# Chained VectorE stages cut into pieces of one link, and all engine orders replaced, in a two-layer gated stack

## The reference

```
x = x + tanh(g_xattn[0]) * L0_xattn(layernorm(x), ctx, mask)      # A
x = x + tanh(g_ffn[0])   * L0_ffn(layernorm(x))                   # F
x = x + tanh(g_xattn[1]) * L1_xattn(layernorm(x), ctx, ctx)       # B
x = x + tanh(g_ffn[1])   * L1_ffn(layernorm(x))                   # R, then the experts
```

## Time and profile before

| what | us |
|---|---|
| median of 3 runs (lowest, highest) | 1640.79 (1635.14, 1644.37) |
| the profiled execution itself | 1642.42 |
| its span, first to last instruction | 1640.8 |
| TensorE busy | 1400.4 (85%) |
| VectorE busy | 1117.3 (68%) |
| ScalarE busy | 993.4 (61%) |
| GpSimd busy | 413.3 (25%) |

### The profile page before, as it was taken

The page is one execution under the profiler, slowest core; times in us unless marked ns, Lnnn a source line. Parts: engine busy times, 40 slices in busy tenths (PEclk is TensorE's granted clock), DMA queues, the critical chain, the costliest instruction groups (busy, mean ns, idle before and its releaser), DMA issues.

```text
span 1640.8 us, 35711 instructions
## 1 busy us (share of the span) xinstructions
PE 1400.4 (85%) x11645; PEld 1072.6 (65%) x11646; DVE 1117.3 (68%) x2887; ACT 993.4 (61%) x2861; POOL 413.3 (25%) x560
## 2 busy tenths in 40 slices
PE   2567789989999889989998671999999999999994
PEld 1445556665666566656664430888888888888883
DVE  7977779899988999899986534344444454444452
ACT  1244778888888888888876760444445444455542
POOL 0101011211122211212111112334433444344442
PEclk9587999999999999999999975999999999999997
DMA  6020132112320223203220005551231412322214
GB/s 192 13 87 30 62 103 103 45 61 104 103 92 21 95 104 103 72 33 104 94 94 8 8 14 179 177 162 32 33 112 30 114 32 35 108 35 32 35 31 123
DMA packets 63158, 123.58 MB, mean 75 GB/s; under 512 B 13955, under 2 KB 51967, under 8 KB 58879
## 3 DMA queue, kind: packets, MB, share of 16 engines
q1 hardware_dynamic: 45743, 102.75, 18.0%
q0 software_dynamic: 17312, 19.56, 7.2%
HBM read 78.64 MB, written 48.04 MB: 77 GB/s over the span
## 4 chain that ended last, share of the span: by engine, by line
PE 52%; DVE 32%; ACT 8%; issue 5%; DMA 2%; POOL 1%; SPq 0%; DVEq 0%; ACTq 0%; POOLq 0%
PE bank L1401 15%; PE bank L1403 14%; PE bank L1402 14%; DVE b_mn L1121 4%; ACT b_ex L746 3%; PE bank L1483 2%; PE bank L1495 2%; DVE wm L1238 1%; DVE f_hs L1182 1%; DVE split_room L1265 1%; DVE wm L1190 1%; PE bank L1719 1%; DVE x L1176 1%; DVE wm L1196 1%; DVE wm L1201 1%
## 5 line engine op out<-in xcount | busy, mean ns | idle before, releaser
L1401 PE MATMUL bank<-split_room,wm 128*128 128x256 f16 x1152 | 314.9, 273 | 8.2 <-issue 6.8
L1378 DVE SCALAR_TENSOR_TENSOR split_room<-bank,b12e,split_room 128x256 f32<-128x256 f32 x288 | 138.2, 484 | 265.6 <-ACT split_room L900 260.8
L1402 PE MATMUL bank<-split_room,wm 128*128 128x256 f16 x1152 | 314.8, 273 | 0.0
L1403 PE MATMUL bank<-split_room,wm 128*128 128x256 f16 x1152 | 314.7, 273 | 0.0
L900 ACT ACTIVATE split_room<-bank,b12e 128x256 f32<-128x256 f32 x288 | 134.2, 470 | 196.0 <-PE bank L1403 194.2
L746 ACT ACTIVATE b_ex<-bank,b_mn 128x120 f32<-128x120 f32 x512 | 177.0, 361 | 36.9 <-DVE b_mn L1121 28.0
L1403 PE MATMUL bank<-wm,split_room 128*128 128x256 f16 x576 | 157.0, 273 | 0.0
L1401 PE MATMUL bank<-wm,split_room 128*128 128x256 f16 x576 | 157.0, 273 | 0.0
L1402 PE MATMUL bank<-wm,split_room 128*128 128x256 f16 x576 | 157.0, 273 | 0.0
L692 POOL DMA_INDIRECT acc<-split_room,m_cur x72 | 116.1, 1612 | 133.0 <-ACT split_room L914 106.1
L1483 PE MATMUL bank<-b_k,b_q 128*128 128x480 f32 x256 | 131.8, 597 | 14.6 <-ACT b_q L834 14.6
(11 more groups left out here) (356 smaller groups left out, 3616.3 us busy)
## 6 DMA issues: line engine op xcount, KB each, us to landing
split_room<-in_L_ffn_W SPq DMA_DIRECT2D x48, 512.0 KB, 8.0
wsplit<-split_room SPq DMA_DIRECT2D x16, 1536.0 KB, 6.6
wm<-wsplit SPq DMA_DIRECT2D x16, 1536.0 KB, 8.5
acc<-x SPq DMA_DIRECT2D x17, 256.0 KB, 2.2
xin<-in_x SPq DMA_DIRECT2D x16, 256.0 KB
rows<-r_row SPq DMA_DIRECT2D x16, 256.0 KB, 3.7
ct<-in_ctx SPq DMA_DIRECT2D x16, 120.0 KB
cb<-in_ctx SPq DMA_DIRECT2D x16, 120.0 KB, 2.6
```

What stands on the lines that cost most here:

```text
L1378: dve.scalar_tensor_tensor(m_h[:, c % 3], bank[c % 4][:, TILE:2 * TILE], b12e[:, p, 1, c:c + 1], m_s[:, c % 2], ALU.add, ALU.mult).then_in ...
L1401: pe.matmul(o, lh, rh, start=start, stop=False)
L1402: pe.matmul(o, ll, rh, start=False, stop=False)
L1403: return pe.matmul(o, lh, rl, start=False, stop=stop)
```

## The change

VectorE's stages that held a chain are cut so that each function holds the operations between two waits. A cut stage's pieces are entries of their own in VectorE's lists: A.ln with A.ln_1, _2, _3; F.ln, B.ln, R.ln with _1, _2; A.rk, A.r0, A.r1, A.p0, A.p1 with _1; F.q becomes F.qa, F.qa_1, F.qa_2, F.qb, and F.q0a, F.q1a get _1, _2; F.qc, F.q0c, F.q1c, F.p, F.p0, F.p1 get _1; R.logit gets _1 to _5; R.rank becomes R.rank_0 to R.rank_5 and R.rank, the last one a wait alone. Operations, operands and waits inside stay as they were. The lists FIRST, ORDER and LAST of all five engines are new. W0 to W2 of batch 15 no longer stand at the end of VectorE's list. The core of the diff, with TensorE's middle list and most of the first and last lists left out:

```diff
-            "ACT": ("A.z@0 A.t@0 A.s0@0 A.s1@0 A.t0@0 A.t1@0 W0@0 A.ot@0 P.n0@0 W1@0 A.z@1 A.t@1 P.n1@0 P.n2@0 P.n3@0 F.z@0 "
...
-            "DVE": ("A.ln@0 P.q0a@0 A.t@0 P.q0b@0 A.rk@0 A.r0@0 A.r1@0 A.s0@0 P.q0c@0 P.q0d@0 A.s1@0 P.q1a@0 P.q1b@0 A.p0@0 "
-                "A.p1@0 P.q1c@0 P.q1d@0 A.ot@0 P.q2a@0 A.out@0 A.ln@1 F.ln@0 P.q2b@0 P.q2c@0 A.t@1 P.q2d@0 A.rk@1 P.n0@0 "
-                "P.n1@0 A.r0@1 A.r1@1 P.n2@0 P.n3@0 P.n4@0 A.s0@1 W0@0 A.s1@1 F.q@0 P.n5@0 P.n6@0 W1@0 A.p0@1 A.p1@1 A.ot@1 "
...
-            "PE": ("A.t@0 A.kv@0 A.q0@0 A.q1@0 A.s0@0 A.s1@0 A.t0@0 A.t1@0 A.p0@0 A.p1@0 A.ot@0 P.n0@0 P.n1@0 A.out@0 A.t@1 "
...
+            "ACT": ("W0@0 P.n0@0 P.n1@0 P.n2@0 A.z@0 W1@0 A.t@0 P.n3@0 P.n4@0 P.n5@0 P.n6@0 A.s0@0 A.s1@0 A.t0@0 A.t1@0 A.ot@0 "
+                "A.z@1 P.n7@0 A.t@1 F.z@0 A.s0@1 F.a@0 A.s1@1 A.t0@1 A.t1@1 F.t@0 A.ot@1 F.gu0@0 F.gu1@0 F.gu2@0 W2@0 F.gu3@0 "
...
+            "DVE": ("P.q0a@0 P.q0b@0 A.ln@0 P.q0c@0 A.ln_1@0 P.q0d@0 P.q1a@0 P.q1b@0 P.q1c@0 P.q1d@0 A.ln_2@0 P.q2a@0 A.ln_3@0 "
+                "P.q2b@0 P.q2c@0 P.q2d@0 P.n0@0 P.n1@0 P.n2@0 A.t@0 P.n3@0 P.n4@0 P.n5@0 P.n6@0 A.rk@0 A.rk_1@0 A.r0@0 "
+                "A.r0_1@0 A.r1@0 A.r1_1@0 A.s0@0 P.b0@0 A.s1@0 A.p0@0 A.p0_1@0 P.b1@0 A.p1@0 A.p1_1@0 A.ot@0 W0@0 A.out@0 "
...
+            "PE": ("P.n0@0 P.n1@0 P.n2@0 A.t@0 P.n3@0 P.n4@0 A.kv@0 P.n5@0 P.n6@0 A.q0@0 P.n7@0 A.q1@0 A.s0@0 A.s1@0 A.t0@0 "
...
         ORDER = {
-            "SP": ("A.load/-1 B.load/1 B.out/3 W/0 R.rank/3").split(),
-            "POOL": ("F.ln/1 B.ln/2 R.ln/3 A.ln/-1 R.scatter/3").split(),
-            "ACT": ("F.a1/2 F.ht0/2 W0/1 B.t2/3 B.s3/3 W1/1 W2/1 B.t3/3 B.s4/3 F.ht1/2 B.s5/3 B.t4/3 B.s6/3 B.rx0/3 A.s0/0 B.r3/3 "
-                "F.z/1 B.t5/3 A.s1/0 B.o0/3 A.t0/0 F.a/1 A.t1/0 B.s7/3 B.t6/3 F.t/1 B.t7/3 B.rx1/3 B.r7/3 B.o1/3 A.ot/0 "
-                "F.gu0/1 B.z/2 B.ct/2 B.zt/2 R.z/3 F.gu1/1 R.t/3 F.gu2/1 A.z/-1 F.gu3/1 B.k/2 B.q/2 A.t/-1 F.a0/1 R.logit/3 "
-                "B.s0/2 B.s1/2 B.t0/2 B.s2/2 B.t1/2").split(),
-            "DVE": ("A.r0/0 B.s5/3 A.r1/0 F.ht1/2 B.s6/3 B.rx0/3 A.s0/0 F.ln/1 W0/1 B.p3/3 W1/1 A.s1/0 F.q/1 B.o0/3 B.s7/3 F.qc/1 "
-                "F.p/1 F.d1/2 A.p0/0 A.p1/0 B.rx1/3 F.t/1 W2/1 B.p7/3 B.ln/2 B.o1/3 A.ot/0 B.out/3 R.ln/3 F.gu0/1 A.out/0 "
-                "B.ct/2 A.ln/-1 F.gu1/1 F.q0a/1 F.gu2/1 B.zt/2 R.t/3 F.gu3/1 F.q0b/1 F.q1a/1 R.logit/3 A.t/-1 B.s0/2 B.v/2 "
-                "F.q0c/1 B.s1/2 F.p0/1 B.s2/2 F.q1b/1 R.rank/3 A.rk/-1 F.q1c/1 B.s3/2 F.p1/1 F.ht0/1 B.s4/2").split(),
...
+            "SP": ("A.load/-1 B.out/3 B.load/0 W/0 R.rank/3").split(),
+            "POOL": ("A.ln/-1 R.ln/3 F.ln/0 R.scatter/3 B.ln/1").split(),
+            "ACT": ("B.t1/3 F.ht0/2 B.t2/3 B.s3/3 F.ht1/2 B.t3/3 W0/1 W1/1 B.s4/3 B.s5/3 F.z/1 A.s0/0 B.t4/3 B.s6/3 B.rx0/3 F.a/1 "
+                "B.r3/3 A.s1/0 A.t0/0 B.t5/3 B.o0/3 A.t1/0 F.t/1 B.s7/3 A.ot/0 B.t6/3 F.gu0/1 B.t7/3 B.rx1/3 W2/1 B.r7/3 "
+                "B.o1/3 F.gu1/1 B.z/2 B.ct/2 F.gu2/1 A.z/-1 F.gu3/1 R.z/3 B.zt/2 F.a0/1 A.t/-1 B.k/2 B.q/2 R.t/3 F.a1/1 "
+                "B.s0/2 B.s1/2 R.logit/3 B.t0/2 B.s2/2").split(),
+            "DVE": ("B.o0/3 A.p0/0 B.s7/3 A.p0_1/0 A.p1/0 A.p1_1/0 F.t/1 B.rx1/3 W1/1 A.ot/0 B.ln/2 B.ln_1/2 B.ln_2/2 F.gu0/1 "
+                "A.out/0 A.ln/-1 B.p7/3 A.ln_1/-1 A.ln_2/-1 B.o1/3 F.gu1/1 A.ln_3/-1 F.q0a/1 B.out/3 F.q0a_1/1 R.ln/3 "
+                "F.q0a_2/1 R.ln_1/3 F.gu2/1 R.ln_2/3 B.ct/2 W2/1 F.gu3/1 F.q0b/1 F.q1a/1 B.zt/2 F.q1a_1/1 F.q1a_2/1 F.q0c/1 "
+                "A.t/-1 F.q0c_1/1 F.p0/1 F.p0_1/1 F.q1b/1 B.s0/2 B.v/2 R.t/3 R.logit/3 R.logit_1/3 F.q1c/1 B.s1/2 R.logit_2/3 "
+                "R.logit_3/3 R.logit_4/3 R.logit_5/3 F.q1c_1/1 A.rk/-1 B.s2/2 R.rank_0/3 R.rank_1/3 A.rk_1/-1 R.rank_2/3 "
+                "B.s3/2 F.p1/1 F.p1_1/1 F.ht0/1 R.rank_3/3 A.r0/-1 A.r0_1/-1 A.r1/-1 A.r1_1/-1 F.ht1/1 B.s4/2 R.rank_4/3 "
+                "B.s5/2 F.ln/0 F.ln_1/0 F.ln_2/0 R.rank_5/3 A.s0/-1 R.rank/3 B.s6/2 B.rx0/2 F.qa/0 F.qa_1/0 F.qa_2/0 F.qb/0 "
+                "W0/0 A.s1/-1 F.qc/0 B.p3/2 F.qc_1/0 F.p/0 F.p_1/0 F.d1/1").split(),
...
         }
...
-                "B.p7@15 B.o1@15 B.out@15 R.ln@15 R.t@15 R.logit@15 R.rank@15 W0@15 W1@15 W2@15").split(),
...
-                "B.s7@14 B.t6@14 B.p5@14 F.d0@15 F.d1@15 B.t7@14 B.p6@14 B.p7@14 B.out@14 B.ct@15 B.zt@15 B.k@15 B.q@15 "
...
+            "SP": ("B.out@13 R.rank@13 B.out@14 R.rank@14 B.out@15 R.rank@15").split(),
...
+                "F.gu1@15 B.z@14 B.ct@14 W2@15 F.gu2@15 B.zt@14 F.gu3@15 R.z@13 F.a0@15 B.k@14 B.q@14 R.t@13 F.a1@15 B.s0@14 "
...
+                "B.s6@14 R.rank_3@13 R.rank_4@13 B.rx0@14 F.d1@15 B.ln@15 B.ln_1@15 B.ln_2@15 B.p3@14 R.rank_5@13 R.rank@13 "
...
+                "R.rank_2@15 R.rank_3@15 R.rank_4@15 R.rank_5@15 R.rank@15").split(),
...
+                "B.s6@14 F.d1@15 B.s7@14 B.p3@14 B.p4@14 B.t5@14 B.t6@14 B.p5@14 B.t7@14 B.p6@14 B.ct@15 B.zt@15 B.p7@14 "
+                "B.out@14 B.k@15 B.q@15 B.v@15 B.s0@15 R.t@14 B.s1@15 R.logit@14 B.t0@15 B.s2@15 B.s3@15 B.p0@15 B.t1@15 "
...
             def variances(G, ch, source):
 
-                def stage(b, p):
-                    x_t, st, rv = G.x[:, p], G.st, G.rv
+                def stats(b, p):
                     ch.start(b)
                     dve.wait_ge(source.done, b + 1)
                     if not isinstance(b, int) or b >= 1:
                         dve.wait_ge(G.rsqrt, b)
                     for t in range(NT):
-                        ch.link(dve.bn_stats(st[:, t, 0:6], x_t[:, t]))
+                        ch.link(dve.bn_stats(G.st[:, t, 0:6], G.x[:, p, t]))
+
+                def moments(b, p):
+                    ch.go_on(b)
                     ch.hold()
                     for t in range(NT):
-                        ch.link(dve.bn_aggr(st[:, t, 6:8], st[:, t, 0:6]))
+                        ch.link(dve.bn_aggr(G.st[:, t, 6:8], G.st[:, t, 0:6]))
+
+                def guard(b, p):
+                    ch.go_on(b)
                     ch.wait()
-                    dve.tensor_scalar(rv[:, 0:NT], st[:, 0:NT, 7], 1e-5, None, ALU.add).then_inc(G.stats, 1)
-                return stage
+                    dve.tensor_scalar(G.rv[:, 0:NT], G.st[:, 0:NT, 7], 1e-5, None, ALU.add).then_inc(G.stats, 1)
+                return stats, moments, guard
...
-            def quantise_a(v, m, sc, b, n):
-                cf.link(dve.tensor_reduce(sc[:, 2], blocks(v), AX.X, ALU.max, apply_absolute_value=True))
-                cf.wait()
-                cf.link(dve.tensor_scalar(sc[:, 0], sc[:, 2], SIXTH, 1e-12, ALU.mult, ALU.max))
-                cf.wait()
-                dve.reciprocal(sc[:, 1], sc[:, 0]).then_inc(F.v, 1)
...
+            def f_largest(n):
+                v, m, sc = F_PARTS[n]
+
                 def stage(b, p):
                     cf.go_on(b)
-                    if part is quantise_a:
-                        dve.wait_ge(F.h, b * 4 + 2 * t + 2)
-                    part(f_h[:, t], f_hm[:, t], f_hs[:, t], b, 1 + t)
+                    if n == 0:
+                        dve.wait_ge(F.z, b + 1)
+                    else:
+                        dve.wait_ge(F.h, b * 4 + 2 * n)
+                    cf.link(dve.tensor_reduce(sc[:, 2], blocks(v), AX.X, ALU.max, apply_absolute_value=True))
+                return stage
+
+            def f_scale(n):
+                v, m, sc = F_PARTS[n]
+
+                def stage(b, p):
+                    cf.go_on(b)
+                    cf.wait()
+                    cf.link(dve.tensor_scalar(sc[:, 0], sc[:, 2], SIXTH, 1e-12, ALU.mult, ALU.max))
+                return stage
...
             def r_logit(b, p):
-
                 cr.go_on(b)
                 dve.wait_ge(R.lg_mm, b + 1)
                 dve.wait_ge(wB_in, 16 * 14)
                 cr.link(dve.tensor_tensor(r_lg[:, :, :], bank[5][:, 0:NT * NE].rearrange("p (t e) -> p t e", t=NT),
                                           br_s[:, :].unsqueeze(1).to_broadcast([P, NT, NE]), ALU.add))
+
+            def r_top_(b, p):
+                cr.go_on(b)
                 cr.hold()
                 for t in range(NT):
                     cr.link(dve.max(r_top[:, t], r_lg[:, t]))
+
```

154 lines of the change are left out of this document (105 added, 49 removed), and 98 rows, old and new, of tables (FIRST, LAST, ORDER).

## The result

The changed kernel takes **1677.74 us** (median of 4, 1675.64 to 1680.79) against 1639.09 for the kernel before in the same comparison (4 runs, 1635.14 to 1644.37): a ratio of **1.0238**, 95% interval 1.0217 to 1.0259. It is slower by 2.4%, where 1623 us (a ratio of 0.99) was forecast and 1643 was the upper end of the range. The profiled execution took 1680.8 us, with a span of 1679.2.

A forecast was written before the change was run, and what follows sets the result against it. TensorE (47.95 us busy) and VectorE (47.34) were taken to bound the 52.28 us step, neither saturated. Steps -21, start +8, drain -4.5 and handover -2 made -19.5 on 1642.4: 1623 us, range 1606 to 1643.

The forecast's parts named there:

- The steps: Eleven steady pipeline steps: each falls from 52.25 to 50.35 us, -21 us in all, bounds 0 and -32.
- busy sums stay: All engines: instructions and shapes are unchanged, so busy times stay and only distances and places move.
- The term of the links: VectorE's steps: 17 links get another piece in front, at 0.11 us each, 1.9 us a step.
- The rule weighed in the prediction: VectorE: the next operation waits for an empty pipe, so covered links give 0; rival of 1644 us, chance 0.05.
- The start: Up to B.out@1: weight preparation ahead of A.t@0 delays F.gu0@0 by 15, partly regained; net +8 us, bounds 0 and +18.
- The -7 for what no longer stands behind: Start, behind F.gu0@0: six pieces P.b, about 8 us together, no longer stand there, -7 us.
- The drain: Batches 13 to 15: B.ct@15 and B.zt@15 earlier on TensorE, plus batch 13's links; -4.5 us, bounds 0 and -9.
- The handover: Before the expert loop: batch 15's split comes earlier, SP sends its weights some 6 us earlier; -2 us, bounds 0 and -6.
- both move the same megabytes: Handover: both kernels load the same amount through the same SP queue, at DMA share 0.55, limiting the gain.
- the wait at L1354 shorter: Handover marker: VectorE's 9.65 us wait for the last split weights should shorten.
- F.z's wait: ScalarE's 1.76 us wait for F.ln's GpSimd operations at F.z: expected gone, booked at 0.
- the Exp load: ScalarE's 1.28 us table load moves from before R.logit to before B.s0; costed 0, otherwise 1.28 us a step.

The follow-up runs named there:

- e4_w2only: Changed kernel with W2 alone moved behind F.q1a in VectorE's step: 1635.6 us, ratio 0.9973.
- e2_oldw2: Kernel before, stages unsplit, with VectorE's W2 moved directly behind R.ln: 1652.4 us, ratio 1.0083.
- e1_split: Changed kernel's cut VectorE stages, with the kernel before's orders on every engine and each stage's pieces side by side: 1640.7 us, ratio 0.9999.
- e3_joinfill: Changed kernel with W2 and F.q0b behind F.q1a, VectorE's stage pieces rejoined (15 borders), B.k's products twice, A.kv's three times: 1693.5 us, ratio 1.0280.
- e3_table: Changed kernel with W2 and F.q0b behind F.q1a, P entries back beside A's stages, Silu in F's gate replaced by a copy: 1646.8 us, one execution.
- e5_both: Changed kernel with P entries back beside A's stages of batches 0 and 1, and W2 alone moved behind F.q1a: 1630.3 us, ratio 0.9906.
- e1_rz: Changed kernel with R.z moved behind B.zt in ScalarE's step, nothing else: 1661.8 us, ratio 1.0131.
- e4_kv: Changed kernel with A.kv's products computed twice on TensorE, nothing else: 1651.8 us, ratio 1.0072.
- e5_start: Changed kernel with P entries back beside A's stages of batches 0 and 1, steps as changed: 1653.0 us, ratio 1.0038.
- e3_w2fill: Changed kernel with W2 and F.q0b behind F.q1a, B.k's products computed twice and A.kv's three times: 1664.3 us, ratio 1.0103.

## Why the prediction was wrong, point by point

**The steps, forecast -21, measured +26.** Two of its own sentences failed.

The first is "W2 moves behind R.ln_2 and may slow R's operations by the same 0.9 us twice; R.z on ScalarE now has F.gu3 in front, which hides it; without that cover 1.8 us on R's chain, on which no later batch waits." The place was right and the size nearly: the two operations are 1.07 and 0.45 us longer. The cover failed: ScalarE was done with F.gu3 and waited 2.15 us. And the last clause was wrong. R's chain is awaited by nobody, but R.z is an **entry in ScalarE's queue**, and B.zt of the batch behind stands right behind it. That is 0.8 us a step (e4_w2only against the 51.9), some 9 us; in the old order the same place costs 1.1 (e2_oldw2 against e1_split).

The second is in the reading of the earlier trace rows, "at a full granted clock", from which TensorE's 47.95 us were taken as fixed ("busy sums stay"). The change leaves TensorE about as much idle time as before, but collects it: before, the longest wait was 0.88 us, after 1.96 and 1.80, with 2.9 us of work between them. The clock falls in every step, in ten of the eleven behind the second wait, and 54.67 less 51.9 is 2.8 us a step, **30 us**, more than all that the steps lost. No rival held this mechanism. VectorE's busy sum didn't stay either (47.34 to 46.16): an operation that starts before its forerunner's end is counted with it.

**The term of the links, 1.9 us a step.** The mechanism was right and the size too large. The kernel without both faults, e4_w2only, has steps of 51.09, 1.2 less than before, where 1.9 was booked; and 0.4 of the 1.2 come with the old orders as well (e1_split), so that 0.8 are left for the new ones. Against the forecast's 50.35 that is another 8 us, and the steps add up: -21 + 9 + 30 + 8 = +26. That covered links are worth something is shown by the other direction: uncovering 15 borders costs 2.4 (e3_joinfill), though a part of it is the pieces' later place. The rule weighed in the prediction (the Trainium skill, VectorE: DVE Perf Modes, "The DRAIN you can't avoid"), by which the semaphore costs nothing extra, is not borne out here: VectorE is busy 1.2 us more in the step with the 15 borders uncovered.

**The start, forecast +8 (0 to +18), measured +13.3.** A.t@0 came at 67.1 (69 forecast), F.gu0@0 at 133.5 (123 forecast), B.out@1 at 282.8 (278). The passes of A with little beside them were sized too short: A.t@0 to A.t@1 is 37.0 us, A.t@1 to F.gu0@0 29.3, where 24 + 8 and 22 were estimated. So F.gu0@0 is 25.5 us later than before, not 15. The -7 for what no longer stands behind was too small as well: from F.gu0@0 to B.out@1 it is 149.3 us for 161.5, -12.2. Two errors of 10 and 5 us took each other back in part, and that 13.3 lies in the range is partly luck.

**The drain, forecast -4.5, measured -1.0.** The clock reads 0.84, 0.86 and 0.82 in its three parts (0.93, 0.96 and 0.76 before). In e4_w2only, with after's last lists word for word, the drain is 134.2, -6.2. Nearly all of the difference lies in the first part, 52.8 us at a clock of 0.84 in after and 47.2 at 0.96 in e4_w2only: the faults of the step reach into the drain, and without them the term was about right. (A drain swings by itself too: e1_split's is 4.4 us longer than before's, with the old lists.)

**The handover, forecast -2, measured 0.** The stretch is 40.3 us in both. The split weights no longer come last on VectorE, and SP sends them 10.1 us behind B.out@15 instead of 15.8, as forecast. But they have landed 28 us behind it in both: VectorE waits 13.20 us for them instead of 9.65, at a DMA share of 0.56 for 0.55. The bound "both move the same megabytes" holds, and the marker "the wait at L1354 shorter" failed.

**The markers.** F.z's wait was gone (0.2 us for 1.76), the Exp load stood ahead of B.s0, covered pieces started 0.1 us before their forerunner's end, as forecast. "A step of 52 or more proves a term wrong" was the one that spoke.

## What to carry to other kernels

A piece that may be slowed is costed on the queue it stands in: not "who waits for its result" but "what stands behind the instruction that waits for it". And on TensorE count idle time by its longest stretches, not by its sum alone: spread over a step of this kernel, 4.3 us cost 4.3; 4.9 us, of which 3.8 lay in two waits, cost 2.9 more in most steps. A search for an order needs a price on both. Two cheap tests find such a loss: repeat some products in the idle stretch (if more work makes it faster, look at the clock), and move one long entry of VectorE by a few places. And before a difference of half a microsecond a step is put down to an order, lay the two steps side by side and find the instruction at which they part: three such differences here (before against e1_split, e3_table, e5_both) came from a late start of ScalarE that no list explains.

## What the runs showed of the hardware

**The granted clock falls after short waits, and not always.** Two waits of 1.96 and 1.80 us with 2.9 us of matmuls between were followed by some 7 us at 0.50; in e1_rz the same 2.08 us wait was followed by a fall in one step and by none in another, for 54.4 and 51.5 us. A short fall behind the first wait cost 0.6 us (e4_kv) or 0.3 (e4_w2only), the long one behind the second 2.9. The Trainium skill, TensorE: Matmul & The Clock Gate, section "HAM oscillation — how this bites in real kernels", describes a kernel in which every wait for a DMA is followed by products at half clock. The trace agrees in kind; here waits of 1.8 to 2.1 us were enough, shorter than those of the page's kernel, and the fall may come in some steps of one order only.

**GpSimd's small operations beside VectorE.** R's root of 128x2 numbers took 0.70 us with VectorE idle (e4_w2only) and 1.77 beside W2, whose two operands lie in SBUF; W2 itself took 1.22 us as ever. In the kernel before it took 0.70 beside F.gu0 and A.out, which read one of their two inputs from PSUM. The Trainium skill, SBUF — State Buffer, section "Who interferes with whom", has VectorE instructions with two SBUF inputs contend with GpSimd instructions that read SBUF; the rows agree with it. It is the rule that would have asked, of each such entry, which GpSimd operation it stands beside.

**A start of ScalarE that is late by half a microsecond.** The same copy, of the same product, started 0.12 us behind its releaser in every step of fourteen kernels and 0.3 to 1.3 us behind it in every step of six. Four of these six (e5_both, e5_start, e3_table, e3_w2fill) have the step order of a kernel that is without it. No run here shows why.
